# A graph network kernel whose edge loops go around once in four turns instead of two (TensorE) or one (ScalarE)

## The chip, the cores and the metric

The kernel runs on one core of one Trainium2 chip. The metric is the device time of one execution in microseconds (us). Engines are named as in the profile: PE is TensorE (PEld its weight loads), DVE is VectorE, ACT is ScalarE, POOL is GpSimd, SP is SyncE. Each engine has a sequencer of its own that reads the engine's instructions in order, handles registers, branches and waits itself, and hands the rest to the engine; in rows of the trace a "q" behind an engine's name (PEldq, ACTq) means that sequencer.

## What is computed

Three layers of message passing over a graph of 3125 nodes and 100000 edges (each used in both directions), 128 features a node and 16 an edge:

```python
for l in range(3):
    e_in = concat([h_prev[s2], h_prev[d2], ef2], axis=-1)
    msg = leaky_relu(e_in @ We1[l]) @ We2[l]
    red = segment_sum(msg, d2, num_segments=3125)
    n_in = concat([h_prev, red], axis=-1)
    out = leaky_relu(n_in @ Wn1[l]) @ Wn2[l]
    h_prev = out + h_prev
x = layernorm(x + out)
```

## The kernel before

**Preparation.** Edges are sorted into buckets of (source block, target block) and written as records to HBM, then turned into feature and number arrays. This takes the first 1200 us and the change does not touch it.

**Tiles, steps, turns.** The edges then lie in tiles of 128. A step handles 3 tiles (`STEP`), a turn 12 steps (`STEPS`). `TURNS` = 31 turns are the most that any input could need; how many this input needs is counted on the chip and read into a register, `live_n`. Each engine has its own program for the edge loop and its own loop over turns, and skips turns beyond `live_n`; the engines meet only at semaphores.

**One step on TensorE** (`step`, L1374 to L1473): for three tiles, one matmul of edge features (L1402) and four gathering matmuls (L1409) into the PSUM regions `gath6` (in tile `sums`) and `gath`; then twelve matmuls (L1470) that scatter the messages of the step three before (`LAG`) into `sums`. The table rows and the places in `sums` are dynamic addresses. In layer 0 they come from words loaded once a turn (`load_words`, L1476) and unpacked in registers; in layers 1 and 2 from rows of `map_row`, loaded every second step (`next_row`). The places of the last steps of a round are needed by the first steps of the next round, so they are loaded into registers of their own (`kept`, `keep_row`, L1558).

**One step on ScalarE** (L804 to L818): copy gath6 to `msg` (L808), clear it (L811), copy gath to `msg` (L813), and make the fp16 upper half of the previous step's message (L817). **One step on VectorE**: leaky relu (L1144), lower half (L1164), and in layer 0 also the one-hot matrices (L1181, L1148) and once a turn a copy (L1170). From layer 1 on the one-hot matrices are read back from HBM by SP's queue.

**The loops.** ScalarE, VectorE and SP go around once a turn: a loop of 31 iterations whose body is under `If(it < live_n)`. TensorE goes around once in two turns: 16 iterations, body under `If(it * 2 < live_n)`, the second turn of a body under `If(it * 2 + 1 < live_n)`; in layers 1 and 2 that inner condition has an Else that loads `kept` three times. Layers 1 and 2 are one outer loop on TensorE (L1542, without a hint) and two copies of the code on the other engines. What "a round" is below: one iteration of TensorE's loop; "an edge": the way from the last instruction of a round to the first matmul of the next.

**After the loop** of a layer ScalarE copies `sums` out bank by bank (L823) once the last sums are in, TensorE computes the node update from it (L1486, L1487, fp32, then L1492), VectorE adds to `hT` (L1223), and TensorE makes the next layer's tables (L1311).

## Time and profile before

| | |
|---|---|
| time, median of 3 runs | 3610.49 us (3607.45 to 3693.87) |
| the profiled execution's own time | 3595.21 us |
| its span, first to last instruction | 3593.5 us |
| PE busy | 2437.8 us (68%) |
| PEld busy | 2105.2 us (59%) |
| DVE busy | 2745.6 us (76%) |
| ACT busy | 2063.7 us (57%) |
| POOL busy | 779.1 us (22%) |
| edge loop of layer 0 | about 1200 to 1997 us |
| edge loop of layer 1 | about 2036 to 2769 us |
| edge loop of layer 2 | about 2810 to 3543 us |

Busy time counts what the engine itself executes, not its sequencer's registers and branches. A busy share over the whole span mixes the preparation, in which VectorE and GpSimd work, with the three edge loops, so the stages are read one by one. Idle time "<-issue" is time in which an engine waited for nothing that the profile shows, that is, for its own sequencer.

### The profile page before, as it was taken

How to read it: one execution, taken by the hardware profiler on the slowest of the kernel's cores; microseconds unless marked ns; L12 is line 12 of the kernel's file. 1: busy time of each engine (PE TensorE's matmuls, PEld its weight loads, DVE VectorE, ACT ScalarE, POOL GpSimd, SP SyncE). 2: the span in 40 equal slices, each digit the busy share in tenths (PEclk: the TensorE clock that was granted, in tenths of full speed). 3: DMA queues.
4: the chain of work that ended last, by engine and by line, in shares of the span. 5: the costliest groups of instructions: out<-in, count | busy, mean ns of one | idle time of the engine just before them, and what ended most of it. 6: DMA issues, size and time to landing. Idle time of an engine off the chain costs nothing.

```text
span 3593.5 us, 80512 instructions
## 1 busy us (share of the span) xinstructions
PE 2437.8 (68%) x26755; PEld 2105.2 (59%) x26756; DVE 2745.6 (76%) x3411; ACT 2063.7 (57%) x4144; POOL 779.1 (22%) x834
## 2 busy tenths in 40 slices
PE   5000000000005899999999899999999999999996
PEld 4000000000004778887878688888887788888885
DVE  8956565656564899999999777777777777777776
ACT  4000000000003678787777688888887688888885
POOL 0477777777775100000000000000000000000000
PEclk9555555555556999999999999999999999999998
DMA  8111111111114777777777455555554355555553
GB/s 252 45 45 45 32 45 32 45 32 45 30 23 123 233 247 257 248 251 254 254 247 254 144 195 193 185 191 193 194 188 171 120 194 189 190 190 194 192 187 121
DMA packets 227338, 563.52 MB, mean 157 GB/s; under 512 B 43272, under 2 KB 124238, under 8 KB 227182
## 3 DMA queue, kind: packets, MB, share of 16 engines
q1 hardware_dynamic: 199758, 547.80, 45.0%
q0 software_dynamic: 27552, 15.37, 2.4%
q8 instruction: 15, 0.25, 0.0%
q14 instruction: 13, 0.11, 0.0%
HBM read 413.11 MB, written 150.16 MB: 157 GB/s over the span
## 4 chain that ended last, share of the span: by engine, by line
PE 49%; POOL 21%; DVE 14%; issue 13%; DMA 1%; SPq 1%; ACT 1%; DVEq 0%; POOLq 0%; ACTq 0%
POOL records L666 21%; PE gath L1409 18%; PE sums L1470 13%; PE sums L1409 9%; PE gath L1402 5%; DVE loop_buf L1164 3%; DVE big L1144 3%; PE sums L1402 2%; DVE loop_buf L1181 2%; DVE gsel L1148 2%; DVE table L1112 1%; DVE table L897 1%; PE sums L1486 1%; PE sums L1487 0%; PE sums L1365 0%
## 5 line engine op out<-in xcount | busy, mean ns | idle before, releaser
L1144 DVE SCALAR_TENSOR_TENSOR big<-big 128x768 f32<-128x768 f32 (+1 forms) x957 | 908.6, 950 | 382.7 <-ACT big L813 356.1
L1409 PE MATMUL gath<-table,gsel 128*128 x7488 | 1074.6, 273 | 0.0
L1164 DVE TENSOR_TENSOR loop_buf<-big,loop_buf 128x768 f16<-128x768 f32 x936 | 890.5, 951 | 0.0
L666 POOL DMA_INDIRECT records<-rec,rowi x784 | 751.5, 959 | 284.1 <-issue 246.8
L1470 PE MATMUL sums<-loop_buf 128*128 128x128 f16 x11232 | 781.2, 219 | 17.0 <-issue 14.1
L1409 PEld LDWEIGHTS gath<-table,gsel 128*128 128x128 f16 x7488 | 733.6, 98 | 84.6
L817 ACT ACTIVATE loop_buf<-big 128x768 f16<-128x768 f32 x936 | 781.4, 835 | 0.0
L813 ACT ACTIVATE big<-gath 128x512 f32<-128x512 f32 x936 | 559.2, 597 | 273.3 <-PE gath L1409 273.3
L1470 PEld LDWEIGHTS sums<-loop_buf 128*128 128x128 f16 x11232 | 650.8, 98 | 105.3 <-ACT sums L811 34.9
L1298 PE MATMUL sums<-table,fchunk 128*128 128x200 f16 x196 | 37.1, 365 | 877.1 <-DVE found L1002 864.6
L1409 PE MATMUL sums<-table,gsel 128*128 x3744 | 563.4, 273 | 13.4 <-DVE gsel L1148 13.4
L1298 PEld LDWEIGHTS sums<-table,fchunk 128*128 128x128 f16 x196 | 24.4, 135 | 889.5 <-issue 886.9
L757 ACT ACTIVATE rec<-big,sc_ef 128x448 f16 x28 | 18.7, 668 | 881.0 <-DMA records<-rec,rowi 881.0
L1402 PE MATMUL gath<-wst,fchunk 128*128 128x256 f16 x1872 | 511.4, 273 | 0.0
L808 ACT ACTIVATE big<-sums 128x256 f32<-128x256 f32 x936 | 352.3, 376 | 102.5 <-PE sums L1409 102.3
L1409 PEld LDWEIGHTS sums<-table,gsel 128*128 128x128 f16 x3744 | 361.5, 98 | 59.4 <-DVE gsel L1148 27.9
L811 ACT ACTIVATE sums<-iota 128x256 f32<-128x256 f16 x936 | 363.0, 388 | 29.7
L699 POOL PARTITION_ALL_REDUCE mxa<-mx x2 | 0.7, 350 | 1577.3 <-DVE mx L1212 1577.3
L1402 PE MATMUL sums<-wst,fchunk 128*128 128x256 f16 x936 | 256.0, 273 | 42.1 <-issue 42.1
L1023 DVE SCALAR_TENSOR_TENSOR rowi<-rowb,rowc 128x28 int32<-128x28 int32 x28 | 5.3, 188 | 326.2 <-DMA records<-rec,rowi 325.9
L1402 PEld LDWEIGHTS gath<-wst,fchunk 128*128 128x128 f16 x1872 | 183.2, 98 | 31.9 <-issue 0.2
L1181 DVE TENSOR_TENSOR loop_buf<-numc,iota 128x768 f16<-128x768 f16 x312 | 172.3, 552 | 3.8 <-DMA ssel_d<-loop_buf 0.2
(188 smaller groups left out, 1641.7 us busy)
## 6 DMA issues: line engine op xcount, KB each, us to landing
gsel<-gsel_d SPq DMA_DIRECT2D x208, 576.0 KB, 3.8
loop_buf<-ssel_d SPq DMA_DIRECT2D x208, 576.0 KB, 5.2
numb<-nums_d SPq DMA_DIRECT2D x106, 576.0 KB, 4.7
gsel_d<-gsel SPq DMA_DIRECT2D x104, 576.0 KB, 5.6
ssel_d<-loop_buf SPq DMA_DIRECT2D x104, 576.0 KB, 6.5
fchunk<-feat_d SPq DMA_DIRECT2D x630, 80.0 KB, 4.6
loop_buf<-rows_d SPq DMA_DIRECT2D x28, 896.0 KB, 4.8
records<-rec,rowi POOLq DMA_INDIRECT x784
```

Of the source, the lines that this page charges most:

```text
L666: pool.indirect_dma_start(out=records[:, :], out_offset=bass.IndirectOffsetOnAxis(ap=rowi[:, h, g:g + 1].bitcast(U32), axis=0), in_=rec[:, ...
L808: act.activation(msg[:, place, 0:2 * D], gath6, ACT.Copy).then_inc(x6_set, 1)
L811: act.activation(gath6, iota[:, 0:2 * D], ACT.Copy, scale=0.0).then_inc(gath6_free, 1)
L813: act.activation(msg[:, place, 2 * D:MSG], gath[:, :], ACT.Copy).then_inc(x_set, 1)
L817: act.activation(m_hi[:, (q - 1) % RING, :], msg[:, (q - 1) % RING, :], ACT.Copy)\
L1144: return dve.scalar_tensor_tensor(m, m, SLOPE, m, ALU.mult, ALU.max)
L1148: dve.tensor_scalar(gsel[:, h, :], numb[:, h, :], part[:, 0:1], None, ALU.is_equal).then_inc(gsel_set[h], DMA)
L1164: dve.tensor_tensor(m_lo[:, place, :], msg[:, place, :], m_hi[:, place, :], ALU.subtract)\
L1181: last = dve.tensor_tensor(ssel[:, t % SLOTS:t % SLOTS + STEP, :, :].rearrange("p t s (e w) -> p (t s) e w", w=2), numc[:, 2 * t:2 * (t + ...
L1402: pe.matmul(uv, fchunk[:, p % PARTS, pair * P:(pair + 1) * P], wst[:, side, :, :].rearrange("p s f -> p (s f)"), start=fresh, stop=False, ...
L1409: return pe.matmul(uv, gsel[:, h, (2 * tc + s) * P:(2 * tc + s + 1) * P], at[n], start=False, stop=n == 3, skip_group_check=True)
L1470: last = pe.matmul(sum_at[i, s], m[:, place, w0:w0 + D], ssel[:, ts, s, :], start=False, stop=False, skip_group_check=True)
```

## The change

TensorE's edge loops now go around once in four turns (`HALVES` = 4, 48 steps), ScalarE's too (before: once a turn), in `ROUNDS` = 8 iterations each. The second, third and fourth turn of a body stand under conditions nested in each other. ScalarE's loop gets the hint at its head. Nothing that an engine executes for a live turn changes; VectorE, SP and GpSimd keep their programs.

```diff
+HALVES = 4
+ROUNDS = -(-TURNS // HALVES)
...
-                with act.Fori(0, TURNS) as it:
-                    with act.If(it < live_n):
-                        step0 = l * live_n * STEPS + it * STEPS
+                def rounds(it, half):
+
+                    turn = it * HALVES + half
+                    with act.If(turn < live_n):
+                        step0 = l * live_n * STEPS + turn * STEPS
                         for q in range(STEPS):
...
+                        if half + 1 < HALVES:
+                            rounds(it, half + 1)
+
+                with nc.Fori(0, ROUNDS, engines=(mybir.EngineType.Activation,), hint_back_edge=True) as it:
+                    rounds(it, 0)
...
-            with nc.Fori(0, -(-TURNS // 2), engines=(mybir.EngineType.PE,), hint_back_edge=True) as it:
-                with pe.If(it * 2 < live_n):
+            with nc.Fori(0, ROUNDS, engines=(mybir.EngineType.PE,), hint_back_edge=True) as it:
+                with pe.If(it * HALVES < live_n):
...
-                                if STEPS - LAG <= q < STEPS:
+                                if q % STEPS >= STEPS - LAG and q < (HALVES - 1) * STEPS:
                                     place = pe.snap(place)
...
-                    take_words(0)
-                    for q in range(STEPS):
-                        step(q, unpacked, step0, turn, it * 2, next_words)
-                    with pe.If(it * 2 + 1 < live_n):
-                        take_words(1)
-                        for q in range(STEPS, 2 * STEPS):
-                            step(q, unpacked, step0, turn, it * 2, next_words)
+                    def rounds(half):
+
+                        take_words(half)
+                        for q in range(half * STEPS, (half + 1) * STEPS):
+                            step(q, unpacked, step0, turn, it * HALVES, next_words)
+                        if half + 1 < HALVES:
+                            with pe.If(it * HALVES + (half + 1) < live_n):
+                                rounds(half + 1)
+
+                    rounds(0)
...
-                        with pe.If(it * 2 + 1 < live_n):
-                            for q in range(STEPS, 2 * STEPS):
-                                step(q, places_at, step0, turn, l * live_n + it * 2, next_row)
-                        with pe.Else():
-                            for j in range(-LAG_LOADS, 1):
-                                keep_row(j, 0)
+                        def rounds(half):
+
+                            for q in range(half * STEPS, (half + 1) * STEPS):
+                                step(q, places_at, step0, turn, l * live_n + it * HALVES, next_row)
+                            if half + 1 < HALVES:
+                                with pe.If(it * HALVES + (half + 1) < live_n):
+                                    rounds(half + 1)
+                                with pe.Else():
+                                    for j in range(-LAG_LOADS, 1):
+                                        keep_row(j, 0)
+
+                        rounds(0)
```

**The end of TensorE's loop in layers 1 and 2.** Before, the last step of a round, then the join, the one Else (L1558, three loads), the count and the closing branch, and the node update behind them:

```order
L1470 MATMUL sums<-loop_buf 128x128 x12
L1589 UNCONDITIONAL_BRANCH
L1558 TENSOR_LOAD map_row x3
L1592 UNCONDITIONAL_BRANCH
L1563 REGISTER_ALU
L1563 COMPARE_AND_BRANCH
L1480 REGISTER_ALU
L1485 ISA
```

And of the changed kernel at the same place:

```order
L1479 MATMUL sums<-loop_buf 128x128 x12
L1604 UNCONDITIONAL_BRANCH
L1570 TENSOR_LOAD map_row x3
L1606 UNCONDITIONAL_BRANCH
L1570 TENSOR_LOAD map_row x3
L1606 UNCONDITIONAL_BRANCH
L1570 TENSOR_LOAD map_row x3
L1606 UNCONDITIONAL_BRANCH
L1575 REGISTER_ALU
L1575 COMPARE_AND_BRANCH
L1489 REGISTER_ALU
```

Each of the three inner conditions now has its own Else, and all three stand behind the last turn's code, so a condition that fails after the second turn jumps over the code of two turns to reach its Else.

**The head and the end of a turn in ScalarE's loop.** Before, the head (names as above: `big` holds `msg`, `loop_buf` the fp16 halves), and the turn's end with the closing branch:

```order
L800 UNCONDITIONAL_BRANCH
L801 COMPARE_AND_BRANCH
L805 ISA
L808 ACTIVATE big<-sums 128x256
...
L817 ACTIVATE loop_buf<-big 128x768
L801 UNCONDITIONAL_BRANCH
L800 REGISTER_ALU
L800 COMPARE_AND_BRANCH
```

Of the changed kernel, the head and the end of the first turn:

```order
L826 UNCONDITIONAL_BRANCH
L826 BRANCH_PREFETCH_HINT
L826 ISA
L805 COMPARE_AND_BRANCH
L809 ISA
L812 ACTIVATE big<-sums 128x256
...
L821 ACTIVATE loop_buf<-big 128x768
L805 REGISTER_ALU
L805 COMPARE_AND_BRANCH
L809 ISA
L812 ACTIVATE big<-sums 128x256
```

Between two turns of a round a condition now stands where the closing branch and the head stood.

## Rows read from the trace of the kernel before

**Rows 1.** Stretches of the edge loops: length, PE, PEld, DVE, ACT, POOL busy (x instructions), clock.
```profile
1400.00:2050.00 650.00, 605.27 (x6558) 509.81 (x6557) 619.05 (x879) 503.62 (x987) 1.11 (x4) 0.99 0.71 239
2100.00:2750.00 650.00, 641.97 (x7495) 575.91 (x7494) 506.65 (x555) 552.94 (x1111) 0.00 (x0) 1.00 0.55 191
```
**Rows 2.** The timeline of PE in layer 1: mid-round, then two edges.
```profile
2120.92 0.83 PE L1470 MATMUL sums<-loop_buf 128*128 128x128 f16 x12
2121.59 0.27 PE L1402 MATMUL sums<-wst,fchunk 128*128 128x256 f16 x1
...
2148.61 0.83 PE L1470 MATMUL sums<-loop_buf 128*128 128x128 f16 x12
2150.18 0.28 PE L1402 MATMUL sums<-wst,fchunk 128*128 128x256 f16 x1 [0.73 <-issue]
...
2206.46 0.28 PE L1402 MATMUL sums<-wst,fchunk 128*128 128x256 f16 x1 [0.73 <-issue]
```
**Rows 3.** PE's sequencer, the closing branch, 2092 to 2207 us: ns min/median/max, first and last.
```profile
L1563 PEldq COMPARE_BRANCH  x3: 234/234/247, 2092.7 to 2205.3; - x3
```
**Rows 4.** The instructions of one line: the copy once a turn on DVE, layer 0.
```profile
L1170 DVE COPY numc<-numcol x26: 224/229/235, 1197.2 to 1968.9; 128x144 f16 x26
```
**Rows 5.** The timeline of DVE in layer 0, around three starts of a turn.
```profile
1539.08 0.23 DVE L1170 COPY numc<-numcol 128x144 f16 x1
...
1569.17 0.23 DVE L1170 COPY numc<-numcol 128x144 f16 x1
...
1570.82 0.96 DVE L1144 SCALAR_TENSOR_TENSOR big<-big 128x768 f32<-128x768 f32 x1 [0.72 <-ACT big L813]
...
1600.41 0.22 DVE L1170 COPY numc<-numcol 128x144 f16 x1
```
**Rows 6.** The timeline at the end of layer 0's loop, ACT and PE.
```profile
1999.19 2.42 ACT L823 ACTIVATE big<-sums,sc 128x512 f32<-128x512 f32 x4 [1.87 <-issue]
...
2000.02 1.10 PE L1486 MATMUL sums<-hT,node_w 128*128 128x512 f32 x2 [2.84 <-ACT big L823]
```
**Rows 7.** Sequencers at loop ends: ACT and PE in layer 0, PE in layer 1.
```profile
L801 ACTq COMPARE_BRANCH  x5: 45/45/50, 1996.5 to 1998.8; - x5
...
L1499 PEldq COMPARE_BRANCH  x4: 92/228/231, 1996.5 to 1999.1; - x4
...
L1589 PEldq COMPARE_BRANCH  x1: 184/184/184, 2767.7 to 2767.7; - x1
```
**Rows 8.** PE's first node matmul of layer 1; the loads of kept rows ahead of it.
```profile
2771.90 1.12 PE L1486 MATMUL sums<-hT,node_w 128*128 128x512 f32 x2 [3.36 <-ACT big L823]
...
L1558 PEldq TENSOR_LOAD <-map_row x3: 847/850/855, 2031.8 to 2033.6; - x3
```
**Rows 9.** Fetches (packets, MB, share): all; 1000-1206; 1206-1262; 1990-2092; 2770 to end.
```profile
q8 instruction: 15, 0.25, 0.0%
...
q8 instruction: 2, 0.03, 0.1%
...
q8 instruction: 5, 0.08, 0.5%
...
q8 instruction: 6, 0.10, 0.4%
...
q8 instruction: 2, 0.03, 0.0%
```
**Rows 10.** Two rounds of layer 1, the first while fetching; landing of a 16 KB transfer.
```profile
2036.00:2092.00 56.00, 56.00 (x634) 49.81 (x633) 41.39 (x46) 46.45 (x94) 0.00 (x0) 0.97 0.50 169
...
2150.10:2206.50 56.40, 55.59 (x649) 49.87 (x650) 43.97 (x49) 47.90 (x97) 0.00 (x0) 1.00 0.55 191
...
nums_d<-numT SPq DMA_DIRECT2D x30, 16.0 KB, 3.5
```
**Rows 11.** The outer loop's branch on PE, and PE's work around it.
```profile
L1542 PEldq COMPARE_BRANCH  x1: 229/229/229, 2786.6 to 2786.6; - x1
...
2784.44 5.54 PE L1492 MATMUL sums<-big,node_w 128*128 128x512 f32 x14
```

More of the change, by code:

```diff
@@ L1498, in _ @@
             start(0)
-            with nc.Fori(0, -(-TURNS // 2), engines=(mybir.EngineType.PE,), hint_back_edge=True) as it:
-                with pe.If(it * 2 < live_n):
-                    step0 = pe.snap(it * (2 * STEPS))
-                    turn = pe.snap(it * (2 * PER_TURN))
+            with nc.Fori(0, ROUNDS, engines=(mybir.EngineType.PE,), hint_back_edge=True) as it:
+                with pe.If(it * HALVES < live_n):
+                    step0 = pe.snap(it * (HALVES * STEPS))
+                    turn = pe.snap(it * (HALVES * PER_TURN))
                     word_of, place_at = {}, {}
@@ L1530, in next_words @@
                         if q % STEPS == STEPS - 1:
-                            load_words(it * (2 * STEPS) + (q + 1))
-                    take_words(0)
-                    for q in range(STEPS):
-                        step(q, unpacked, step0, turn, it * 2, next_words)
-                    with pe.If(it * 2 + 1 < live_n):
-                        take_words(1)
-                        for q in range(STEPS, 2 * STEPS):
-                            step(q, unpacked, step0, turn, it * 2, next_words)
+                            load_words(it * (HALVES * STEPS) + (q + 1))
+                    def rounds(half):
[6 more added lines that the diff above has]
+                    rounds(0)
             node(0)
@@ L1556, in keep_row @@
                 def keep_row(j, turn_n):
-                    pe.reg_load(kept[-j % (2 * LOADS)], row_words(j, turn_n))
+                    pe.reg_load(kept[-j % (HALVES * LOADS)], row_words(j, turn_n))
                 for j in range(-LAG_LOADS, 1):
@@ L1562, in _ @@
                 start(l)
-                with nc.Fori(0, -(-TURNS // 2), engines=(mybir.EngineType.PE,), hint_back_edge=True) as it:
-                    with pe.If(it * 2 < live_n):
-                        step0 = pe.snap(l * live_n * STEPS + it * (2 * STEPS))
-                        turn = pe.snap((l * live_n + it * 2) * PER_TURN)
+                with nc.Fori(0, ROUNDS, engines=(mybir.EngineType.PE,), hint_back_edge=True) as it:
+                    with pe.If(it * HALVES < live_n):
+                        step0 = pe.snap(l * live_n * STEPS + it * (HALVES * STEPS))
+                        turn = pe.snap((l * live_n + it * HALVES) * PER_TURN)
                         loaded = {}
@@ L1571, in next_row @@
                             j = (q + 1) // LOAD_STEPS
-                            if q % LOAD_STEPS == LOAD_STEPS - 1 and j < 2 * LOADS - LAG_LOADS:
+                            if q % LOAD_STEPS == LOAD_STEPS - 1 and j < HALVES * LOADS - LAG_LOADS:
                                 _, loaded[j] = nc.values_load_multi_w_load_instructions(
-                                    row_words(j, it * 2), engines=(mybir.EngineType.PE,),
+                                    row_words(j, it * HALVES), engines=(mybir.EngineType.PE,),
                                     min_val=0, max_val=(NB - 1) * NODE_BYTES,
@@ L1577, in next_row @@
                             elif q % LOAD_STEPS == LOAD_STEPS - 1:
-                                keep_row(j, it * 2)
+                                keep_row(j, it * HALVES)
                         def places_at(t):
@@ L1583, in places_at @@
                             row_at = loaded.get(j) or [bass.RuntimeValue.of_register_unchecked(r)
-                                                       for r in kept[-j % (2 * LOADS)]]
+                                                       for r in kept[-j % (HALVES * LOADS)]]
                             return [bounded(place) for place in row_at[k:k + 2]]
-                        for q in range(STEPS):
-                            step(q, places_at, step0, turn, l * live_n + it * 2, next_row)
-                        with pe.If(it * 2 + 1 < live_n):
-                            for q in range(STEPS, 2 * STEPS):
-                                step(q, places_at, step0, turn, l * live_n + it * 2, next_row)
-                        with pe.Else():
-                            for j in range(-LAG_LOADS, 1):
-                                keep_row(j, 0)
+                        def rounds(half):
[8 more added lines that the diff above has]
+                        rounds(0)
                 node(l)
```

## The prediction

> **What bounds the kernel now.** I read the busy times by stage first, then the timeline of one engine at a time, then the sequencers' own records at the places where the timeline shows a hole. In layer 0 the engine to watch is DVE: 619.05 of 650 us, PE 605.27. From layer 1 on it is PE: 641.97 of 650 us, DVE 506.65, ACT 552.94 [rows 1]. Layer 2 has the same pattern as layer 1, so one price serves both. The clock is granted in full (0.99 and 1.00), so no clock effect enters.
>
> In layer 1 a step begins 0.67 us after its predecessor's sums began (2120.92 to 2121.59, mid-round). At the end of a round it is 1.57 us (2148.61 to 2150.18), with 0.73 us idle "<-issue": PE waits for its own sequencer [rows 2]. An edge thus costs 1.57 - 0.67 = 0.90 us, and edges recur every 56.28 us (2150.18 to 2206.46). Part of it is the closing branch, taken in 234 ns [rows 3]; the hint and the head's registers are the rest. The row at 2121 is within a round, and no step anywhere inside a round shows the hole, the one behind the inner condition (L1589) included: a condition that holds is not taken and costs PE nothing in layers 1 and 2, because matmuls already queued cover it.
>
> DVE makes its copy of once a turn 26 times in layer 0 [rows 4]. So 26 turns are live, in each layer: 13 rounds of two turns, 12 edges between them, and 3 empty rounds (16 - 13). Of ACT's 31 iterations 5 are empty. The changed kernel has 7 live rounds on both engines (the last holds two turns), 6 edges, and one empty round (8 - 7).
>
> **Term 1, edges in layers 1 and 2.** 6 fewer in each, 2 x 6 x 0.90 = **10.8 us** off. PE is the bound and nothing else is late there: ACT and DVE have 15% and 22% of the time idle, so a PE that comes 0.90 us earlier meets no new wait.
>
> **Term 2, edges in layer 0.** Here DVE bounds, so I price by DVE. A turn that begins behind a single-turn boundary lasts 1569.17 - 1539.08 = 30.09 us; one that begins behind an edge lasts 1600.41 - 1569.17 = 31.24 us, and its first L1144 waits 0.72 us for ACT, which waits for PE [rows 5]. An edge costs DVE 1.15 us, and 6 x 1.15 = **6.9 us** come off. The 30.09 us remain as DVE's own work; I do not take more.
>
> **Term 3, ACT's edges.** They cost nothing now: ACT's sequencer branches while ACT executes L817, and steps at ACT's boundaries inside a PE round keep their 0.67 us [rows 2]. Having fewer of them gains nothing. The new hint and conditions lie in the same cover.
>
> **Term 4, the end of layer 0.** ACT starts L823 at 1999.19 after 1.87 us "<-issue" [rows 6], so it was done with the last step at 1997.32: that is its five empty iterations [rows 7]. PE's three empty rounds run beside them, four closing branches from 1996.5 to 1999.1, so (1999.1 - 1996.5) / 3 = 0.87 us each. PE begins the node update at 2000.02, when the first L823 is done [rows 6]. In the changed kernel both engines have one failed condition, one closing branch back, one empty round and the exit. ACT would be through by about 1997.4 and its first L823 done 0.7 us later, 1998.1. PE would be through at about 1996.4 + 0.3 (failed condition) + 0.87 + 0.2 = 1997.8. If nothing else happens the node matmuls start near 1998.2, 1.8 us earlier.
>
> **Term 5, the ends of layers 1 and 2.** Here the failed condition has an Else. Live turns are even in number, so before it never ran: 13 x 2 = 26. Now the third condition of the seventh round fails, and PE's sequencer makes three loads of 0.85 us, 0.91 us apart (1.8 us from first to third start) [rows 8], 2.7 us in all. PE reaches L1589's place at 2767.7 [rows 7]; + 0.3 + 2.7 + 0.3 (out of the Else) + 0.87 + 0.5 (exit, head of the node update) = 2772.4, against 2771.90 before. **0.5 us later** each, if nothing else happens; ACT, ready by 2770.0, no longer sets it.
>
> **Term 6, fetching code.** One round is 649 matmuls and 650 weight loads [rows 10]. PE fetches code by q8: 15 packets and 0.25 MB in the whole execution, 16 KB each: 2 from 1000 to 1206 us, 5 in the first round of layer 0, 6 from the end of layer 0 through the first round of layer 1, 2 behind the loop of layer 1 [rows 9]. That makes up the 15: none falls into a later round. So now the two-turn body stays resident, with the rest of the outer loop, and no branch has ever waited for code. The two-turn body is 5 to 6 packets, so the four-turn body is about 11. Whether that much stays resident, no row shows. Streaming it in order is free: in the 56 us of layer 1's first round, in which code was fetched, PE was busy for 56.00 [rows 10]. What may not be free is a jump to code that is not there: the failed condition over two turns' code (5 to 6 packets), once a layer; and the closing branch.
>
> A late fetch is bounded below by the packet's own time, 0.5% of 16 engines over 56 us for 5 packets, 0.9 us [rows 9], and above by the 3.5 us from issue to landing of a 16 KB transfer [rows 10]. I take 2 us, between them, and I take it that the failed jump misses and the hinted closing branch does not, since the hint names its target 110 us ahead. Then layer 0's node matmuls start at 1997.8 + 2 = 1999.8 instead of 2000.02 (0.2 off), and layers 1 and 2 lose 0.5 + 2 = 2.5 each. The outer branch L1542 has no hint, but runs at 2786.6 while PE has matmuls queued to 2789.98 [rows 11]: up to 3.4 us of cover, so I price it at nothing; uncovered it would be 2 us once.
>
> **Sum:** -10.8 - 6.9 - 0.2 + 5.0 = -12.9 us. Against the profiled execution's 3595.21 that is 3582.3. The median of the runs is 15.3 us higher, and the edges are the same in each, so I take the difference from it: 3610.49 - 12.9 = **3597.5 us**.
>
> **Rivals.**
> (A) All code is there, jumps too: layer ends give -1.8 + 2 x 0.5 = -0.8, the sum is -17.7 - 0.8 = -18.5, 3592. For it: no jump has stalled yet. Against it: the body is larger than anything shown resident. Chance 0.25.
> (B) The other side: the hinted closing branch comes late too, in 18 edges. At 0.9 us each that is 16.2 and the time is 3614; at 3.5 us it is 63 and 3660. It decides from 12.9 / 18 = 0.7 us an edge. For it: the hint has never had anything to fetch in this trace, since the body was resident. Against it: 110 us of notice, and a packet takes about 1. Chance 0.2. The Trainium skill (Runtime: NRT & Kernel Launch, Instruction fetch mechanics) gives TensorE room for 2048 instructions in 16 KiB blocks of 256 and says that a taken branch outside the window stalls on a fetch; by that rule the old body (649 + 650 and its registers) fits, and the trace agrees; the new one, twice that, does not fit, and (B) is what it would do here if the hint failed. The same section says the window is two blocks; the trace disagrees, as a body of five packets was never fetched again.
> (C) The conditions inside a round cost what the edges cost, or PE's earlier arrival is eaten in layer 0 by DVE: nothing moves, 3610. Against it the mid-round rows, where a condition costs nothing. Chance 0.1.
>
> **How the numbers follow.** The forecast has 0.45 and, with late jumps between 0.9 and 3.5 us, spans -16 to -8, 3594 to 3602. The range reaches down to (A) with some drift between runs, 3587, and up past (C) and the cheap half of (B), 3617, leaving the dear half of (B) out. Faster or slower by 2% would be 72 us, about what a measurement of this kernel can tell from no change; no case reaches it but (B) at more than 4.7 us an edge, or an effect I have not seen. So faster 0.01, within 2% 0.96, slower 0.03.
>
> **What would show it.** PE in layer 1: holes "<-issue" only every 111.7 us, of 0.73 us still (terms 1, 6); larger ones there mean (B). DVE in layer 0: turns of 30.09 three in four. L1486's successor about 2.5 us later behind the last sums in layers 1 and 2, about level in layer 0; earlier there means (A). The instruction queue's packets rise from 15 to some 80 per layer if the body does not stay resident, and to some 25 in all if it does. If spans fall by far more or less than 13 us with edges as forecast, the layer ends or ACT's larger body are mis-sized.

## The result, and the profile after

| | before | after |
|---|---|---|
| median of the timed runs | 3610.95 us | 3637.59 us |
| range of the runs | 3607.45 to 3693.87 | 3633.96 to 3724.30 |
| ratio after / before | | 1.0076, 95% interval 1.0062 to 1.0091 |
| span of the profiled execution | 3593.5 us | 3635.9 us |
| code packets fetched for TensorE (q8) | 15 | 249 |

The changed kernel is slower by 26.6 us where 12.9 us less were forecast, and 3637.59 lies above the range that was given. One of the five executions of before and two of after fell into a slower state, 2.3 to 2.4% above the others; the ratios, here and below, leave such executions out, and without them the medians are 3610.7 and 3635.4 us, 24.7 apart. The profiled executions are 42.4 us apart. 14.3 us of that lies ahead of the first edge step: it starts at 1213.92 us, and at 1199.58 us in the trace of before. The preparation is the same code in both, and its end lay anywhere from 1199 to 1218 us in the profiles of this study, those without the change included. The other 28.1 us is the change, in one profile of each kernel, and agrees with the timed difference (the interval of the ratio is 22 to 33 us).

Where it went can be read from two things that PE does in each layer, its first step (L1411, before L1402) and its first node matmul (L1495, before L1486). The timeline of PE after (start, length in us, what it is, in brackets the idle time before it and what ended it):

```profile
1213.92 0.28 PE L1411 MATMUL sums<-wst,fchunk 128*128 128x256 f16 x1 [1.46 <-issue]
...
2011.03 1.10 PE L1495 MATMUL sums<-hT,node_w 128*128 128x512 f32 x2 [1.04 <-ACT big L832]
...
2049.23 0.39 PE L1411 MATMUL sums<-wst,fchunk 128*128 128x256 f16 x1 [3.59 <-issue]
...
2794.39 2.07 PE L1495 MATMUL sums<-hT,node_w 128*128 128x512 f32 x2 [8.73 <-issue]
...
2837.62 0.39 PE L1411 MATMUL sums<-wst,fchunk 128*128 128x256 f16 x1 [3.64 <-issue]
...
3585.05 2.07 PE L1495 MATMUL sums<-hT,node_w 128*128 128x512 f32 x2 [10.90 <-issue]
```

and those of before that no group above shows (the others are in [rows 6, 8]):

```profile
1199.58 0.34 PE L1402 MATMUL sums<-wst,fchunk 128*128 128x256 f16 x1
...
2035.84 0.39 PE L1402 MATMUL sums<-wst,fchunk 128*128 128x256 f16 x1 [3.76 <-issue]
...
2809.46 0.39 PE L1402 MATMUL sums<-wst,fchunk 128*128 128x256 f16 x1 [3.56 <-issue]
...
3545.77 2.07 PE L1486 MATMUL sums<-hT,node_w 128*128 128x512 f32 x2 [3.27 <-ACT big L823]
```

| from, to | before | after | difference |
|---|---|---|---|
| layer 0, first step to node matmul | 800.44 | 797.11 | -3.3 |
| layer 0, node matmul to layer 1's first step | 35.82 | 38.20 | +2.4 |
| layer 1, first step to node matmul | 736.06 | 745.16 | +9.1 |
| layer 1, node matmul to layer 2's first step | 37.56 | 43.23 | +5.7 |
| layer 2, first step to node matmul | 736.31 | 747.43 | +11.1 |
| layer 2, node matmul to the end of the span | 47.73 | 50.85 | +3.1 |

The sum is +28.1. The loops of layers 1 and 2 themselves (first step to last step) grew by 3.7 and 3.5 us of these (730.23 to 733.96, 730.57 to 734.07); layer 0's got shorter by 1.5. The rest, 22 us, is behind them.

**The end of layer 1.** PE starts its last twelve sums at 2784.83 and its first node matmul at 2794.39. PE's sequencer in between (instruction, count, ns min/median/max, first and last start), the lines L1604 (third condition), L1570 (loads of the Else) and L1575 (loop):

```profile
L1604 PEldq COMPARE_BRANCH  x1: 3849/3849/3849, 2784.9 to 2784.9; - x1
...
L1570 PEldq TENSOR_LOAD <-map_row x3: 847/864/867, 2788.8 to 2790.6; - x3
...
L1575 PEldq COMPARE_BRANCH  x2: 92/800/1508, 2791.9 to 2794.1; - x2
```

The failed condition takes 3.85 us. The same line takes 74 ns where its condition holds:

```profile
L1604 PEldq COMPARE_BRANCH  x22: 74/74/203, 2164.0 to 2756.5; - x22
```

The three loads take 2.7 us as forecast, and the closing branch behind them 1.51 us, against 234 ns in [rows 3]. In layer 2 these two branches take longer together, 3.36 and 4.17 us:

```profile
L1604 PEldq COMPARE_BRANCH  x1: 3360/3360/3360, 3573.4 to 3573.4; - x1
...
L1575 PEldq COMPARE_BRANCH  x2: 92/2133/4174, 3579.9 to 3584.7; - x2
```

**Behind the first node matmul** there is a second hole, 2.90 us in layer 1, with nothing late but PE's own sequencer; before had none there. And the granted clock is at half, the 1.2 GHz level, from 2789 to 2806 us, where before it was so for 3.4 us, from 2773 to 2777. The timeline of PE and the stretches (as in rows 1: length, PE, PEld, DVE, ACT, POOL busy, granted clock, DMA share, GB/s) of after:

```profile
2800.22 1.01 PE L1496 MATMUL sums<-big,node_w 128*128 128x512 f32 x1 [2.90 <-issue]
...
2804.44 1.81 PE L1495 MATMUL sums<-hT,node_w 128*128 128x512 f32 x2
...
2806.95 1.02 PE L1495 MATMUL sums<-hT,node_w 128*128 128x512 f32 x2
```
```profile
2788.50:2794.40 5.90, 0.01 (x1) 0.01 (x1) 0.00 (x0) 1.81 (x4) 0.00 (x0) 0.54 0.46 143
...
2800.20:2806.10 5.90, 5.88 (x8) 2.29 (x8) 2.13 (x4) 1.20 (x2) 0.00 (x0) 0.51 0.01 3
2806.10:2812.00 5.90, 5.90 (x15) 2.66 (x14) 4.13 (x7) 1.79 (x3) 0.00 (x0) 1.00 0.00 0
```

and of before behind its first node matmul:

```profile
2772.00:2778.00 6.00, 6.00 (x11) 2.48 (x12) 1.42 (x3) 4.08 (x8) 0.00 (x0) 0.72 0.26 97
```

The clock falls while PE stands idle for 8.73 us. At 0.51 a pair of fp32 node matmuls takes 1.81 us, at 1.00 it takes 1.02 us. Before had only 3.36 us idle [rows 8], and the clock of the 6 us behind it was 0.72.

**The edges.** An edge in layer 1 now has 0.89 us of idle where it had 0.73 [rows 2], since its closing branch takes 372 ns instead of 234; and once a round a step in mid-body waits 0.45 us for the sequencer. PE's timeline, then the closing branch:

```profile
2165.69 0.28 PE L1411 MATMUL sums<-wst,fchunk 128*128 128x256 f16 x1 [0.89 <-issue]
...
2278.25 0.28 PE L1411 MATMUL sums<-wst,fchunk 128*128 128x256 f16 x1 [0.89 <-issue]
2329.28 0.84 PE L1479 MATMUL sums<-loop_buf 128*128 128x128 f16 x12 [0.45 <-issue]
...
2391.06 0.28 PE L1411 MATMUL sums<-wst,fchunk 128*128 128x256 f16 x1 [0.90 <-issue]
```
```profile
L1575 PEldq COMPARE_BRANCH  x6: 366/372/389, 2164.4 to 2727.7; - x6
```

A round of four turns takes 112.56 us (2165.69 to 2278.25), exactly two rounds of two turns of before (2 x 56.28). The next takes 112.81. So going around half as often brought nothing. The first four turns, in which the body runs for the first time, even take 116.46 us (2049.23 to 2165.69) where before took 114.34 (2035.84 to 2150.18): 2.1 of the 3.7 us by which layer 1's loop grew lie there. Code is now fetched all the time: 12 packets in one round, about what the whole body was estimated to be (queue, packets, MB, share of 16 engines).

```profile
q8 instruction: 12, 0.20, 0.7%
```

### The profile page after: what moved, and what is told of

Same layout as the page of the kernel before. It is cut to its first block, busy times and chain, and to the rows that moved or that the text cites. A ratio compares the mean times of both kernels' runs of the same rounds, so it can differ in the third digit from the quotient of the medians.

```text
span 3635.9 us, 80191 instructions
## 1 busy us (share of the span) xinstructions
PE 2444.9 (67%) x26755; PEld 2105.7 (58%) x26756; DVE 2744.9 (75%) x3411; ACT 2066.3 (57%) x4144; POOL 782.6 (22%) x834
## 4 chain that ended last, share of the span: by engine, by line
PE 50%; POOL 19%; DVE 13%; issue 13%; DMA 2%; ACT 1%; SPq 1%; another core or an unknown queue 0%; DVEq 0%; POOLq 0%; ACTq 0%
POOL records L668 19%; PE gath L1418 18%; PE sums L1479 14%; PE sums L1418 9%; PE gath L1411 5%; DVE big L1153 3%; DVE loop_buf L1173 3%; PE sums L1411 2%; DVE loop_buf L1190 2%; DVE gsel L1157 1%; DMA ssel_d<-loop_buf 1%; DVE table L1121 1%; PE sums L1495 1%; PE sums L1496 1%; DVE table L906 1%
## 5 line engine op out<-in xcount | busy, mean ns | idle before, releaser
L1411 PE MATMUL gath<-wst,fchunk 128*128 128x256 f16 x1872 | 511.8, 273 | 0.0
L1411 PE MATMUL sums<-wst,fchunk 128*128 128x256 f16 x936 | 256.0, 274 | 35.6 <-issue 35.6
L1411 PEld LDWEIGHTS gath<-wst,fchunk 128*128 128x128 f16 x1872 | 183.2, 98 | 35.6 <-issue 2.1
```

Of the source, the lines that this page charges most:

```text
L1411: pe.matmul(uv, fchunk[:, p % PARTS, pair * P:(pair + 1) * P], wst[:, side, :, :].rearrange("p s f -> p (s f)"), start=fresh, stop=False, ...
```

## The experiments

All numbers are ratios to the kernel before on the same chip, with 95% intervals; the runs were made on several chips. A profile is one execution of each kernel. "Gap" is the time from a layer's last step to the next layer's first; before has 41.68 and 43.39 us, and 53.48 us from the last step to the end.

### One part at a time

`a1_act`: the kernel before with the change of ScalarE's loop alone. `a2_pe`: the change of TensorE's loops alone. `a3_l0`: ScalarE's, and TensorE's in layer 0 alone.

Against after, `a2_pe` has the old loop on ScalarE, and `a3_l0` the old one on TensorE in layers 1 and 2:

```diff
-                with nc.Fori(0, ROUNDS, engines=(mybir.EngineType.Activation,), hint_back_edge=True) as it:
-                    rounds(it, 0)
+                with act.Fori(0, TURNS) as it:
+                    with act.If(it < live_n):
...
-                with nc.Fori(0, ROUNDS, engines=(mybir.EngineType.PE,), hint_back_edge=True) as it:
-                    with pe.If(it * HALVES < live_n):
+                with nc.Fori(0, -(-TURNS // 2), engines=(mybir.EngineType.PE,), hint_back_edge=True) as it:
+                    with pe.If(it * 2 < live_n):
```

> The kernel before with the change made on ScalarE alone (four turns a round, hint); TensorE goes around once in two turns as before. Theory (code fetch on TensorE is the whole loss): TensorE's body stays resident, so no step changes. Only ScalarE's empty iterations at a layer's end shrink, and there TensorE's three empty rounds now decide: 0 to 1 us off in each of three layers, ratio 0.999 to 1.000. Rival (ScalarE's longer body is fetched or branches late): slower by 3 us or more, with holes of ScalarE at its edges.

Measured: 1.0001 (0.9992 to 1.0010).

> The changed kernel with ScalarE's old loop: TensorE's part of the change alone. Theory (TensorE's code fetch): the whole loss is here, ratio 1.007 to 1.009 of before, and the first node matmul of layers 1 and 2 again comes about 9 us behind the last sums. Rival (the two parts need each other): under 1.004.

Measured: 1.0054 (1.0041 to 1.0068), 249 packets; the gaps are 44.78 and 54.91, the last stretch 63.96 us.

> Four turns a round on TensorE in layer 0 only, two in layers 1 and 2; ScalarE as changed. Theory (the loss sits at the ends of layers 1 and 2 and in their rounds): nothing of it is left, and layer 0 keeps what it gained in the changed kernel, about 1.5 us in the loop, so ratio 0.998 to 1.001; the first node matmuls of layers 1 and 2 within 1 us of before. Rival (layer 0 loses too, outside what the single traces show): over 1.002.

Measured: 0.9998 (0.9989 to 1.0007), 87 packets; gaps 42.27 and 40.86.

Most of the loss is TensorE's (19.6 of 24.7 us; 1.007 to 1.009 was expected), and lies in layers 1 and 2. ScalarE's part costs nothing measurable alone, but not for lack of effect: in `a1_act`, in the first round of layers 1 and 2 one step comes 1.16 and 0.82 us later, PE waiting for ACT 23 us into the layer,

```profile
2060.39 0.84 PE L1479 MATMUL sums<-loop_buf 128*128 128x128 f16 x12 [0.99 <-ACT sums L815]
```

where ACT comes to its new code for the first time, and the last stretch shrinks by 3.6 us. ACT's fewer empty iterations give 0.7 of that ahead of the node matmul, which starts after 2.53 us of idle instead of 3.27. The other 2.9 lie behind it, with the clock: before it stood at half from 3544.7 to 3551.5 us, and the first pair of node matmuls took 2.07 us; here it stays at 1.00, and the pair takes 1.12. Layer 0's part, with its six fewer edges, gains 2 us in its loop (794.57 to 792.52), and that is not to be seen in the time.

### A full last round

26 turns end in the middle of a body of four. `e28_before` and `e28_after` add two turns over empty tiles to the count (8% more steps), so that the last round is full and no inner condition fails.

```diff
-    float(STEP * LAG)
+    float(STEP * LAG + 2 * ITER)
```

> The kernel before, made to run 28 turns a layer in place of 26 (empty tiles in the last two): two more turns in each of three layers, 1 more round, 61 + 2 x 56 = 174 us more, ratio 1.048. It is the base for the next.

Measured: 1.0479 (1.0461 to 1.0496), 15 packets.

> The changed kernel, made to run 28 turns a layer: 7 full rounds, so no condition in a round fails, no Else runs, nothing jumps over two turns' code; an empty round remains at the end. Theory (most of the loss is that jump, the three loads behind it and the slow clock after them): against the kernel before with 28 turns it loses under 10 us, and TensorE's idle time ahead of the first node matmul of layers 1 and 2 is under 5 us. Rival (the loss comes with any end of a loop whose code was not resident): 8 us idle there as before, 20 us lost.

Measured: 1.0512 (1.0491 to 1.0533), 262 packets. The medians, taken as for the ratios, are 3781.1 and 3794.9 us, 13.8 us apart and not 24.7, though not under 10 as expected. In the profiles, from the first edge step to the end, it is 13.4 us for 28.1. The loops are now level or better (854.25 against 855.24, 786.16 against 786.56, 786.23 against 786.66), and PE's first node matmul comes as early as anywhere, 3.8 us after the last step starts. But the next piece of the node update is late by more, 4.64 us in layer 1 and 7.40 us in layer 2:

```profile
2905.72 1.12 PE L1495 MATMUL sums<-hT,node_w 128*128 128x512 f32 x2 [1.33 <-ACT big L832]
2911.92 0.59 PE L1496 MATMUL sums<-big,node_w 128*128 128x512 f32 x1 [4.64 <-issue]
...
3747.11 1.01 PE L1496 MATMUL sums<-big,node_w 128*128 128x512 f32 x1 [7.40 <-issue]
```

So 11 to 15 us of the loss, about half of it in the loops and half behind them, go with the incomplete last round. The gaps are still 2.0 and 4.0 us longer than those of `e28_before`, and the last stretch 9.3 (15.3 us for 22.4): code behind the loop is fetched behind the exit, where `e28_before` has no such hole. That it must be so for a body of this size does not follow; `g_four_slot0` below has the body of after and no such loss behind its loops.

### Is it the size, or the jump?

`f_dead` puts code that never runs into the loop of before: 700 matmuls (about 1400 instructions with their weight loads) under a condition that never holds, behind the second turn, in layers 1 and 2. `f_dead_short` has 60.

```diff
+    with pe.If(it + live_n < 2):
+        for dead in range(DEAD_MATMULS):
+            pe.matmul(gath[:, 0:P], zeros16[:, 0:P], zeros16[:, 0:P], ...)
```

> The kernel before with 700 matmuls that never run at the end of TensorE's round in layers 1 and 2, under a condition that is false in every round: edges, rounds and work as before, one more taken branch a round, over code as long as two turns. Theory (code that does not stay resident is what costs): fetches on q8 rise from 15 to some 100 or more, a jump over the dead code stalls about 3.8 us as the one in the changed kernel did; if in all of 26 rounds, 90 to 110 us slower, ratio 1.02 to 1.03. Rival (the long stall in the changed kernel came from its three loads or its other Else branches): 0.3 us a round more, 8 us, 1.002.

Measured: 1.0037 (1.0023 to 1.0051), 26 packets.

> The same with 60 matmuls under the condition in place of 700: the same branch is taken, the code stays short. Both theories: fetches on q8 stay near 15, the branch itself costs 0.2 to 0.4 us a round, 5 to 10 us in all, ratio 1.001 to 1.003. If it is as slow as with 700, the length of the code is not the cause.

Measured: 1.0019 (1.0008 to 1.0029), 24 packets.

The jump over 700 matmuls is late once and then never. The branch in the first round, and in the second:

```profile
L1593 PEldq COMPARE_BRANCH  x1: 3313/3313/3313, 2110.2 to 2110.2; - x1
...
L1593 PEldq COMPARE_BRANCH  x1: 245/245/245, 2171.4 to 2171.4; - x1
```

and in `f_dead_short` 0.59 us the first time; layer 2 shows the same once more (the medians are 3622.5 and 3614.0 us, and the late jump with the 1.7 us behind it accounts for most of that). From 2200 to 2600 us `f_dead` fetches nothing at all, where some 100 packets or more in all were expected and 26 measured. So once the target is there the distance of a jump costs nothing, and code that lies in a loop and isn't executed does not bring fetches into every round. What counts there is the code that is executed in a round. Around the outer loop it was otherwise: before fetched nothing in layer 2's loop, `f_dead` 6 packets and `f_dead_short` 5. The added branch with 60 unexecuted matmuls was enough for the body not to stay from layer 1 to layer 2.

### Without the hint, and with three turns

`b1_nohint` is after without `hint_back_edge` on both engines. `a4_three` has `HALVES = 3` (and 16 more words in a row of numbers, which the body's reads need), so a body of three quarters of the size.

```diff
-            with nc.Fori(0, ROUNDS, engines=(mybir.EngineType.PE,), hint_back_edge=True) as it:
+            with nc.Fori(0, ROUNDS, engines=(mybir.EngineType.PE,)) as it:
```
```diff
-HALVES = 4
+HALVES = 3
```

> The changed kernel without the hint at the head of TensorE's and ScalarE's loops. Theory (four turns' code does not stay, the hint has the head fetched ahead of the closing branch): each of 6 edges a layer stalls some 3.5 us more, 18 edges, 50 to 65 us slower than the changed kernel, 1.021 to 1.026 of before. Rival (the hint does nothing, the branch finds its target anyway): 0.1 us an edge faster than the changed kernel, 1.007.

Measured: 1.0321 (1.0306 to 1.0337), 271 packets.

> Three turns a round on both engines (11 iterations, 9 live rounds, the last of two turns), the rest as changed. Its code for TensorE is about 8 packets of 16 KB. Theory (what executes in a round must stay, with the outer loop's other code): it does not quite fit either, q8 fetches some 60 to 80 a layer, and at the ends of layers 1 and 2 the failed condition and its loads come as in the changed kernel; ratio 1.002 to 1.007. Rival (three turns fit): q8 stays near 25, 4 edges a layer saved, ends as before, 0.997 to 1.000.

Measured: 1.0468 (1.0452 to 1.0484), 270 packets. The closing branch in layer 1 (first `b1_nohint`, then `a4_three`), and the edge of `a4_three` on PE's timeline:

```profile
L1575 PEldq COMPARE_BRANCH  x3: 3430/3590/3910, 2298.8 to 2533.2; - x3
```
```profile
L1575 PEldq COMPARE_BRANCH  x4: 2706/3114/3226, 2250.8 to 2527.4; - x4
...
2254.89 0.28 PE L1411 MATMUL sums<-wst,fchunk 128*128 128x256 f16 x1 [3.79 <-issue]
2259.38 0.82 PE L1418 MATMUL gath<-table,gsel 128*128 x3 [3.39 <-issue]
```

Without the hint a closing branch to code that isn't there costs 3.59 us, with the hint in after 0.37 us. That is what the hint is worth on the branch. The whole kernel lost more than the 50 to 65 us expected against after, about 88: the three loops grew by 23 to 26 us each, 4 us an edge, and the gap behind layer 0 by 10 us (52.55 for 42.27). But with three turns the hinted branch is as late as one without a hint, and the block behind the head is late again, 7.2 us of idle in one edge. The smaller body is worse than the larger one, and three turns are still too much to stay. Size alone does not decide what an edge costs.

### Where the head stands

The code is fetched in blocks of 16 KB [rows 9]. The head of the loop may lie anywhere in its block. Four kernels differ from `a4_three` or from after only in that TensorE's loop heads are moved to a given place in the block, slot 0 or slot 128.

```diff
-engines=(mybir.EngineType.PE,), hint_back_edge=True) as it:
+engines=(mybir.EngineType.PE,), hint_back_edge=True, head_slot={mybir.EngineType.PE: 0}) as it:
```

> Three turns a round with both of TensorE's loop heads placed at the start of a 16 KB block of code; nothing else differs from the kernel with three turns (1.047), whose edges stalled twice, 3.8 us ahead of the head's first matmul and 3.4 us ahead of a matmul a little behind it. Theory P (where the head lies in a block decides whether the hinted fetch covers the head): the stalls change by over 2 us an edge, ratio under 1.03. Rival S (the number of blocks in a round alone decides): 1.04 to 1.05 again.

Measured: 1.0067 (1.0049 to 1.0085).

> The same with the heads in the middle of a block. Theory P: the head's block holds half as much of the head as with the start of a block, so the next block is needed sooner; stalls differ from those with the start of a block by over 1 us an edge. Rival S: no difference from it beyond 0.3%.

Measured: 1.0135 (1.0117 to 1.0153).

> The changed kernel with TensorE's loop heads at the start of a block. Theory P: the step behind an edge (0.3 us in the changed kernel) loses its wait, as the next block is 256 instructions away, and ends of layers may change, ratio 1.003 to 1.007. Rival S: 1.0076 within its interval.

Measured: 3659 and 3662 us, against 3610 of before, 1.014; from two executions alone, so without an interval.

> The changed kernel with the heads in the middle of a block. Theory P: waits behind an edge of 0.3 us or more, ratio at or above that with the start of a block by up to 0.01. Rival S: the same as it.

Measured: 1.0129 (1.0110 to 1.0147).

The closing branch of the loop of layers 1 and 2, in the order `g_three_slot0`, `g_three_slot128`, `g_four_slot0`, `g_four_slot128`:

```profile
L1575 PEldq COMPARE_BRANCH  x5: 1021/1144/1474, 2224.3 to 2564.6; - x5
```
```profile
L1575 PEldq COMPARE_BRANCH  x5: 366/372/386, 2258.5 to 2595.0; - x5
```
```profile
L1575 PEldq COMPARE_BRANCH  x3: 2936/3063/3272, 2279.3 to 2512.1; - x3
```
```profile
L1575 PEldq COMPARE_BRANCH  x3: 392/464/467, 2309.1 to 2533.8; - x3
```

and that of layer 0's loop (L1508), where the two with slot 128 are late (`g_three_slot128`, then `g_four_slot128`):

```profile
L1508 PEldq COMPARE_BRANCH  x8: 1877/2701/3454, 1306.7 to 1975.6; - x8
```
```profile
L1508 PEldq COMPARE_BRANCH  x6: 3072/3558/3957, 1334.1 to 1966.9; - x6
```

Between 2200 and 2600 us `a4_three`, `b1_nohint` and the two kernels of three turns with a moved head fetch 43 or 44 packets each, after 41: all fetch the body anew in each round, in nearly the same amount. Only when the head arrives differs. Moving it took the three-turn edge in layer 1 from 3.1 us on the branch to 0.37, and the four-turn one from 0.37 to 3.1, so placement decides whether a hint is in time. But no slot is good as such: with three turns slot 128 is in time in layer 1 and late in layer 0, and with four turns slot 0 is late in layer 1. The placement decides the exits as well. `g_four_slot0` has the body of after, and its third condition, which fails over the same two turns' code, is in time in layers 1 and 2; so is the closing branch behind its Else (0.24 us in layer 1). PE's first node matmul then comes 6.38 us after the last step starts, 0.55 later than before, and there is no hole in the node matmuls behind it:

```profile
L1604 PEldq COMPARE_BRANCH  x1: 248/248/248, 2805.0 to 2805.0; - x1
...
2809.74 1.97 PE L1495 MATMUL sums<-hT,node_w 128*128 128x512 f32 x2 [3.91 <-ACT big L832]
```

Its two gaps and last stretch are 40.40, 45.36 and 52.95 us, together as long as those of before; its whole loss lies in the loops (1.2, 24.3 and 25.2 us). In `g_four_slot128` the same condition takes 5.09 us in layer 1 and 0.24 in layer 2, though it is one piece of code. Where the head, the closing branch and the loop's end stand in their blocks relative to each other, and what was executed before them, would have to be varied apart, and that stays open.

### The empty rounds, and a version that beats both

If the empty rounds and their outer conditions are what a layer's end costs, then they can be had without a larger body. `d_both` is the kernel before with loop ends in a register, so that no empty round and no outer condition exists on either engine. `d_all` does the same for VectorE too, `d_both_nohint` is `d_both` without the hint on TensorE.

```diff
+    live_r = pe.snap((live_n + 1) // 2)
...
-    with nc.Fori(0, -(-TURNS // 2), engines=(mybir.EngineType.PE,), hint_back_edge=True) as it:
-        with pe.If(it * 2 < live_n):
...
+    with nc.Fori(0, live_r, engines=(mybir.EngineType.PE,), hint_back_edge=True) as it:
...
-    with act.Fori(0, TURNS) as it:
-        with act.If(it < live_n):
+    with act.Fori(0, live_n) as it:
```

> The kernel before, rounds of one and two turns as before, but both loops end at the number of live rounds (a register) in place of 31 or 16 with a condition around the body: no empty rounds, one branch less an edge on TensorE. Theory (edges and empty rounds cost what the rows of before showed): 36 edges cheaper by the 0.14 us of that branch are 5 us, and the ends of three layers come 1.8 us earlier each, 5.4 us; ratio 0.996 to 0.998. Rival (a loop end in a register costs the same as the condition, or the layer's end is bound elsewhere): 0.999 to 1.001.

Measured: 0.9959 (0.9946 to 0.9973), 15 packets.

> As the kernel that ends TensorE's and ScalarE's loops at the number of live rounds (measured 0.9959), and VectorE's loops too. VectorE's branches lie behind its own work, so theory: no change beyond 1 us, ratio 0.995 to 0.997. If VectorE's edge cost it time in layer 0, where it is the bound, 26 turns become up to 0.1 us shorter each, 0.995.

Measured: 0.9956 (0.9943 to 0.9970).

> Rounds of two turns that end at the number of live rounds, as measured before at 0.9959, and no hint. The two-turn body stays resident, so the hint has nothing to fetch. Theory: an edge loses one instruction of the head, 0.09 us in 36 edges, 3 us faster, ratio 0.995. Rival (the hint keeps the head's code from being late even here): edges of 1 us more, slower than with it.

Measured: 0.9944 (0.9930 to 0.9958), 15 packets; the fastest of this study, 3575.74 us.

PE begins the node update 3.8 us after the last step starts, where before needed 5.8, with 1.33 us of idle instead of 3.36, and the clock stays at 1.00. The end of layer 1 in `d_both`, its timeline and the stretch behind:

```profile
2766.84 1.12 PE L1486 MATMUL sums<-hT,node_w 128*128 128x512 f32 x2 [1.33 <-ACT big L822]
```
```profile
2766.84:2772.80 5.96, 5.96 (x14) 2.77 (x15) 2.78 (x5) 4.68 (x9) 0.00 (x0) 1.00 0.61 220
```

The gaps and the last stretch fall to 39.51, 39.48 and 48.69 us, 10.9 us together. And with the outer condition and its registers gone an edge has 0.56 us idle instead of 0.73, and 0.38 without the hint (an edge of `d_both`, then one of `d_both_nohint`):

```profile
2148.90 0.28 PE L1402 MATMUL sums<-wst,fchunk 128*128 128x256 f16 x1 [0.56 <-issue]
```
```profile
2202.66 0.28 PE L1402 MATMUL sums<-wst,fchunk 128*128 128x256 f16 x1 [0.38 <-issue]
```

The intervals of the two overlap, but the loops of layers 1 and 2 are 2.3 and 2.5 us shorter in the profile, 12 edges of 0.18 us and a little more. So the hint on a loop whose code stays is pure cost here, 0.18 us of idle an edge; in after it was worth 3.2 us on the branch.

## Why the prediction was wrong, point by point

Between the forecast (-12.9 us) and the profiles (+28.1) lie 41.0 us. 18.0 of them are term 1's (forecast -10.8, the loops of layers 1 and 2 +7.2), 5.4 are term 2's (-6.9, layer 0's loop -1.5), and 17.5 lie at the layers' ends, terms 4 to 6 (+4.8, measured +22.3). One step of the prediction is behind the ends and over half of term 1 (`a2_pe`, without ScalarE's part, misses the forecast of the two loops by 9.9 us): term 6 allowed that the body does not stay, and priced that at one late jump of 2 us a layer and at nothing everywhere else.

**Term 1, edges in layers 1 and 2: the price of an edge was right, the price of the edges that stay was not.** The 0.90 us of before is measured rightly, and six fewer are gone. But the first four turns of layer 1, one edge fewer, took 2.1 us more instead of 0.9 less (mostly ACT's first pass through its new code, since `a2_pe` took 114.20 us for them and before 114.34). And each edge that stays costs 1.06 us at the edge, 0.3 to 0.4 in the step behind it and 0.45 to 0.6 in mid-body, about 1.9 and 2.1 us over a round of four turns in layers 1 and 2, where two edges of before cost 1.8. The prediction took the old price for a body that was no longer the old one, though its own term 6 said that the body might not stay. The loops of layers 1 and 2 were to get shorter by 5.4 us each and got longer by 3.7 and 3.5. With TensorE's part alone (`a2_pe`) it was about 1.6 us a round, the loops at 729.33 and 730.55: level. That after then has some 4 us a layer more is beyond the 1 us that ScalarE's part costs alone. In layer 1, 2.3 of it are in the first four turns; the rest, in the rounds behind, was not settled, and since `e28_after` has the body of after and level loops, it may be no more than how one execution differs from another.

**Term 2, layer 0: mechanism right, size wrong.** The start of a turn on DVE, as in [rows 5]:

```profile
1459.39 0.23 DVE L1179 COPY numc<-numcol 128x144 f16 x1
1461.32 0.96 DVE L1153 SCALAR_TENSOR_TENSOR big<-big 128x768 f32<-128x768 f32 x1 [1.01 <-ACT big L817]
1491.02 0.23 DVE L1179 COPY numc<-numcol 128x144 f16 x1
1521.22 0.22 DVE L1179 COPY numc<-numcol 128x144 f16 x1
1551.45 0.22 DVE L1179 COPY numc<-numcol 128x144 f16 x1
1581.79 0.22 DVE L1179 COPY numc<-numcol 128x144 f16 x1
```

The turns last 31.63, 30.20, 30.23 and 30.34 us, 122.40 together. Forecast were three of 30.09 and one of 31.24, 121.51; before had 122.66. So an edge less gave 0.26 us instead of 1.15, and six gave 1.5 instead of 6.9. Two readings failed: the edge that stays is dearer (1.01 us of wait for 0.72), and 30.09 us was not DVE's steady turn but the one after a long one; a turn among short ones takes 30.2 to 30.3.

**Term 3, ScalarE:** nothing, as forecast, to within 3.6 us.

**Term 4, the end of layer 0:** between the two cases. The jump found its target, so PE reaches its node matmul 4.07 us after the last step starts, not 5.86, the 1.8 us that was given for that case. Then the node update has a hole of 2.09 us and the gap ends 0.6 us longer (forecast 0.2 shorter). The late thing was priced at the jump, which took 0.24 us, and came behind it. Why the jump over two turns' code is in time here and late in layers 1 and 2 is open; `g_four_slot0` shows that it is not its length.

**Term 5, the Else:** its three loads took 2.7 us, as worked out, and where nothing else is late (`g_four_slot0`) PE comes to its node matmul 0.55 us later than before, the 0.5 us of this term.

**Term 6 is the step that failed, in the rounds as told under term 1, and at the ends in four ways.** It had one late jump of 2 us at the end of each of layers 1 and 2, 2.5 us with term 5. The gaps grew by 11.0 and 10.7. In layer 1, first node matmul: 5.4 us later (11.2 after the last step starts, for 5.8). First, the failed branch took 3.85 us instead of 2, above the upper bound of 3.5. Second, the closing branch, named as never late since its hint comes 110 us ahead, took 1.51, and 4.17 in layer 2: here it is reached from the Else, right behind a late jump. The Else alone does not undo the hint, since `g_four_slot0` goes through it and takes 0.24 us; whether the late jump does, no run tells. Third, the next block in line is late as well, 2.90 and 2.37 us. Streaming in order had been called free from a stretch in which PE was busy throughout [rows 10]; behind a late jump PE had nothing left to do. Fourth, the clock falls in the idle time, where the prediction had said that no clock effect enters, from stretches inside the loops. Of the 5.6 us by which the node update of layer 1 is longer (18.16 for 12.54, up to the matmuls behind it [rows 8, 11]), 2.7 are not the hole; in them the same matmuls run at half clock. The outer branch was covered nearly as predicted: it takes 3.60 us at 2814.7, under matmuls that last to 2818.09, and PE idles 0.51 us. (Of the two packets that term 6 put behind layer 1's loop one lies behind layer 2's, at 3562 us; nothing hangs on that.)

```profile
L1554 PEldq COMPARE_BRANCH  x1: 3597/3597/3597, 2814.7 to 2814.7; - x1
```
```profile
2812.55 5.54 PE L1501 MATMUL sums<-big,node_w 128*128 128x512 f32 x14
2818.59 3.72 PE L1320 MATMUL sums<-wts,hT 128*128 x16 [0.51 <-issue]
```

**The rivals.** (A) fell at once: 249 packets. (B) was given as dearer hinted branches in every edge, and in after that is 0.14 us a branch (0.37 for 0.23) instead of 0.9 to 3.5; its price is what `a4_three` and `g_four_slot0` paid. So (B) was right about the sign and not about the place: its sum of 18 late hints is not what after shows. The forecast's own figure of packets, some 80 a layer, was right (249 in three layers). What stayed was a round with 1299 matmuls and weight loads; rounds of three turns (1949) and of four (2598) did not, each with register instructions on top that are not counted here. The rule of the Trainium skill (Runtime: NRT & Kernel Launch, Instruction fetch mechanics), room for 2048 instructions, agrees with that if those of three turns are 100 or more. The fetches say that they are: the 77 packets of layer 1's loop in `g_three_slot0` are about 9 for a round of three turns, and by the Trainium skill's 256 instructions a block (same section) the room is 8, an estimate from its figures. The Trainium skill's statement in the same section that the window is two blocks is contradicted, since 15 packets served a whole execution with a body of five.

## What to carry to other kernels

Before a loop body is unrolled further, count the instructions that its engine executes in a round, weight loads too, and look whether the profile's code packets rise beyond the first round: as long as they don't, an edge has one price; where they did, the edges, the exits and what stands behind the loop all got new ones, which moving the loop's head changed by some 3 us an edge and 5 to 7 us an exit. Price the exit of a loop by everything that is late in a row (the failed jump, the branch back, the next block, and the clock after the idle time), not by one fetch. An empty round and its condition are best removed by a loop end in a register, which here gave 0.4% at no cost, and on the loop whose code stays the hint only cost.

## What the runs showed of the hardware that was not expected

- A branch to code that is not there mostly took 3.3 to 3.9 us on TensorE's sequencer (3.85, 3.36, 3.60, 3.59 and 3.31 us in the rows above, and up to 5.3 in `g_four_slot128`), three to five times the 1.05 us that a packet takes (0.7% of 16 engines over 112.5 us for 12 packets).
- Code that is not executed did not make a loop's rounds fetch: 700 dead matmuls in it cost one late jump a layer. Around the outer loop a branch over 60 was enough for 5 packets in layer 2's loop, where before had none.
- A hinted branch that is in time costs 0.37 us, not the 0.23 of resident code, and whether it is in time depends on where the head lies (0.37 or 3.1 us for the same loop moved by part of a block). So does whether the jump out of an incomplete round is in time (3.85 or 0.25 us).
- In the 8.73 and 10.90 us of idle the granted clock fell to half and stayed there for 17 us each time; with 1.33 us of idle it stayed at 1.00. In layer 2 of before, 6.8 us at half behind 3.27 us of idle went with 2.9 us more up to the end than in `a1_act`, where the clock stayed at 1.00.
